# A fused attention and expert kernel whose first two tiles run interleaved, with a third start-up step of its own

## The reference, cut to what matters

```python
q, k, v = sigmoid(x @ Wq + bq), sigmoid(x @ Wk + bk), x @ Wv + bv       # by head
sink_in = normal / sum_d(q * cumsum(k)); src_out = normal / sum_d(k * cumsum(q))
cons_sink = sum_d(q * cumsum(k * src_out)) / normal
cons_src = clip(sum_d(k * cumsum(q * sink_in)) / normal, -1, 1)
vs = v * exp(cons_src) / cumsum(exp(cons_src)) * normal
kv = cumsum(outer(k, vs)); a = (q * sink_in / normal) . kv * sigmoid(cons_sink)
h = LN0(x + a @ Wo + bo); x1 = LN1(h + gelu(h @ W1 + b1) @ W2 + b2)
x2 = LN2(x + x1)
out = LN3(x2 + sum_e gate_e(x2) * (relu(x2 @ wi + bi + x2 @ A_e @ B_e) @ wo + bo))
```

## Time and profile before

| quantity | value |
|---|---|
| timed runs, median | 419.21 us (419.05 to 419.9) |
| the profiled execution, its own time | 418.39 us |
| its span in the trace | 416.6 us |
| PE (TensorE) busy | 374.6 us, 90% |
| DVE (VectorE) busy | 327.9 us, 79% |
| POOL (GpSimd) busy | 223.2 us, 54% |
| ACT (ScalarE) busy | 216.6 us, 52% |
| granted TensorE clock, mean | 0.99 |

### The profile page before, as it was taken

How to read it: one execution, slowest core, us unless ns; L and a number is a source line. 1 busy time by engine, 2 the same in 40 slices (tenths; PEclk the granted TensorE clock), 3 DMA queues, 4 the chain that set the end, 5 groups by cost and what they waited for, 6 DMA issues and landing times.

```text
span 416.6 us, 6454 instructions
## 1 busy us (share of the span) xinstructions
PE 374.6 (90%) x2082; PEld 261.3 (63%) x2082; DVE 327.9 (79%) x787; ACT 216.6 (52%) x399; POOL 223.2 (54%) x263
## 2 busy tenths in 40 slices
PE   8897789788998999989998999899989997799991
PEld 3555556465756875677657774778478765775551
DVE  3649966599589988999799979997899889832632
ACT  2240226327853586538852795278644874175541
POOL 2017234983279527963497348942795369735211
PEclk9999999899999999999999999999999999999997
DMA  8236006400180007300560028000810063000000
GB/s 257 115 71 158 1 2 152 125 3 0 37 217 2 0 2 183 97 0 2 116 162 2 0 56 223 3 0 16 204 36 0 2 160 68 0 1 27 12 14 25
DMA packets 19857, 26.58 MB, mean 64 GB/s; under 512 B 1648, under 2 KB 9968, under 8 KB 19824
## 3 DMA queue, kind: packets, MB, share of 16 engines
q1 hardware_dynamic: 19680, 25.96, 24.5%
q10 hardware_dynamic: 144, 0.21, 0.3%
HBM read 7.29 MB, written 2.10 MB: 23 GB/s over the span
## 4 chain that ended last, share of the span: by engine, by line
PE 31%; DVE 27%; POOL 19%; issue 14%; DMA 5%; ACT 2%; SPq 0%; POOLq 0%; DVEq 0%; ACTq 0%
POOL prod L848 12%; PE pB L354 5%; DMA vb<-vs 5%; DVE kv L1037 5%; PE pY L428 4%; PE pG L421 3%; DVE cum_kv L1043 3%; DVE cum_ks L937 2%; PE pG L497 2%; POOL rstd L838 2%; PE pG L490 2%; DVE cum_q L937 2%; PE pY L508 2%; DVE cum_qs L937 2%; DVE gel L1141 2%
## 5 line engine op out<-in xcount | busy, mean ns | idle before, releaser
L848 POOL TENSOR_TENSOR prod<-cum_kv,q_fac 128x512 f32<-128x512 f32 x64 | 94.5, 1483 | 33.9 <-DVE cum_kv L1043 25.7
L404 PEld LDWEIGHTS pO<-s_wor,prod 128*128 128x128 f32 x512 | 62.2, 191 | 33.5 <-POOL prod L848 21.4
L404 PE MATMUL pO<-s_wor,prod 128*128 128x128 f32 x512 | 69.5, 281 | 14.0 <-POOL prod L848 13.9
L1037 DVE TENSOR_TENSOR kv<-k,vb 128x512 f32<-128x512 f32 x64 | 52.8, 825 | 6.7 <-DMA vb<-vs 6.7
L835 POOL TENSOR_TENSOR var_eps<-mv,s_con 128x4 f32<-128x4 f32 x32 | 9.9, 310 | 71.1 <-DVE mv L1063 71.1
L1043 DVE TENSOR_TENSOR_SCAN cum_kv<-p_ones,cum_kv,kv 128x512 f32<-128x512 f32 x32 | 40.5, 1275 | 0.6
L1043 DVE TENSOR_TENSOR_SCAN cum_kv<-p_ones,kv 128x512 f32<-128x512 f32 x32 | 38.5, 1213 | 0.5
L657 ACT ACTIVATE v<-pA,s_att 128x512 f32<-128x512 f32 x7 | 4.8, 687 | 62.9 <-PE pA L340 62.9
L754 ACT ACTIVATE relu<-pG,s_att 128x512 f32<-128x512 f32 x28 | 19.2, 684 | 27.4 <-PE pG L490 27.4
L508 PEld LDWEIGHTS pY<-s_moe,gel 128*128 128x128 f32 x256 | 30.7, 192 | 3.7 <-issue 1.9
L508 PE MATMUL pY<-s_moe,gel 128*128 128x128 f32 x256 | 32.6, 276 | 0.0
(11 more groups left out here) (164 smaller groups left out, 772.7 us busy)
## 6 DMA issues: line engine op xcount, KB each, us to landing
vb<-vs SPq DMA_DIRECT2D x64, 256.0 KB, 4.7
xT<-x_t SPq DMA_DIRECT2D x8, 256.0 KB, 4.3
xt<-x SPq DMA_DIRECT2D x8, 256.0 KB, 5.3
out<-y SPq DMA_DIRECT2D x8, 256.0 KB, 2.3
s_moe<-moe_w SPq DMA_DIRECT2D x1, 836.0 KB, 10.4
s_wor<-wo_rep SPq DMA_DIRECT2D x1, 512.0 KB, 8.2
s_ffn<-ffn_w SPq DMA_DIRECT2D x1, 512.0 KB, 8.9
s_con<-consts SPq DMA_DIRECT2D x1, 502.0 KB, 4.4
```

Source lines behind the costliest of these rows:

```text
L404: mm = pe.matmul(pO3[:, s, :], prod[:, m % 4, s * P:(s + 1) * P], s_wor[:, m, :], start=False, stop=(m == DH - 1), skip_group_check=True)
L848: pool.tensor_tensor(prod[:, m % 4, :], cum_kv[t.par][:, m, :], q_fac[t.par][:, :], ALU.mult).then_inc(prod_ready, 1)
L1037: dve.tensor_tensor(kv[:, m % 3, :], k[t.par][:, :], vb[:, m, :], ALU.mult).then_inc(kv_ready, 1)
```

## The change

Tile 1's projections get banks of their own (pG[1] for q, pM for k and its first head sums), so its front need not wait for that of tile 0. The start now has three parts of its own. `opening` has tile 0's front and the beginning of tile 1's (up to its inverse denominators). `second_step` has the rest of tile 1's front beside tile 0's outer products, and no FFN. `third_step` has tile 2's front, tile 1's outer products, the FFN of tile 0 and that of tile 1, and tile 0's gate and first experts. It also takes over tile 2's outer products up to `outer_product(2, 5)` and `product(2, 2)`, which step 2 leaves out (`b.n > 2`). The common `step` begins at s=2. Tile 2's input is loaded at the end of the list of first transfers rather than later. Ten waits are added so that tiles interleaved in shared buffers don't overwrite each other. The fillers become 27 where there were 30.

```diff
+        def q_bank(t):
+            return pG[1] if t.n == 1 else pA
+        def k_bank(t):
+            return pM if t.n == 1 else pB
...
                 sp.wait_ge(vs_ready, t.n + 1)
+                wait(sp, kv_ready, DH * (t.n - 1) + m + 1)
...
+            load_xT(Tile(2))
...
             def project_q(t):
-                wait(pe, qfac_ready, t.n)
+                if t.n > 1:
+                    pe.wait_ge(qfac_ready, t.n)
...
             def project_v(t):
-                if t.n > 0:
+                if t.n == 1:
+                    pe.wait_ge(qfac_ready, t.n)
+                elif t.n > 1:
                     pe.wait_ge(q_ready, t.n + 1)
...
             def second_step(b):

                 a = b.plus(1)
+                keep_busy(1)
+                reduce_out(b, 1); reduce_out(b, 2)
+                keep_busy(1)
+                head_sums(a, 1, True)
+                reduce_out(b, 3)
+                keep_busy(1)
+                head_sums(a, 1, False)
...
+            def third_step(c):
+
+                b, a = c.plus(1), c.plus(2)
+                project_q(a); project_k(a)
...
+            def third_step(c):
+
+                b, a = c.plus(1), c.plus(2)
+                q_out(a); k_out(a)
+                normalise(c, 0); v_out(a); seed_x(b); h_out(c)
+                gelu(c, 0); gelu(c, 1)
+                seed_h(c)
+                gelu(c, 2); gelu(c, 3)
...
+                if B and b.n > 2: product(b, 1); product(b, 2)
...
-            step(Tile(-1))
+            opening(Tile(0))
             second_step(Tile(0))
-            run_steps(step, first=1, end=TILES)
+            third_step(Tile(0))
+            run_steps(step, first=2, end=TILES)
```

More of the change, by code:

```diff
@@ L312, in step @@
                 if B: spread_vs(b, 4); spread_vs(b, 5); spread_vs(b, 6)
-                if A and a.n == 2: load_xT(a)
                 if A and a.n >= 1: load_xt(a)
@@ L351, in head_sums @@
                 src, at = (kq, HW) if of_q else (qk, 0)
+                dst = k_bank(t) if pair == 0 else pB
                 for s in reversed(range(SUB)):
                     end = base + at + (s + 1) * HEADS
[L354 removed]
+                    mm = pe.matmul(dst[:, end - P:end], src[:, s * P:(s + 1) * P], wide_sum, start=True, stop=True)
                 mm.then_inc((den_ready, consp_ready)[pair], 1)
@@ L552, in second_step @@
                 a = b.plus(1)
+                keep_busy(1)
[3 more added lines that the diff above has]
+                reduce_out(b, 3)
+                keep_busy(1)
+                head_sums(a, 1, False)
+                reduce_out(b, 4)
                 keep_busy(2)
-                for m in range(1, 5):
-                    reduce_out(b, m)
-                head_sums(a, 0, True); head_sums(a, 0, False); project_v(a)
@@ L928, in _ @@
             second_step(Tile(0))
-            run_steps(step, first=1)
+            third_step(Tile(0))
+            run_steps(step, first=2)
         @block.vector
@@ L1174, in closing, with opening @@
                 expert_residual(c); moments(c, 3)
+            def opening(a):
+                b = a.plus(1)
+                cumulate_q(a); cumulate_k(a); k_times_cum_q(a, 0); q_times_cum_k(a, 0)
+                inverse_denominators(a); normal_denominators(a)
+                cumulate_q(b)
+                sink(a); cumulate_sink(a); source(a); k_times_cum_q(a, 1); cumulate_source(a); q_times_cum_k(a, 1)
+                cumulate_k(b)
+                k_times_cum_q(b, 0)
+                conserved(a); clip_source(a)
+                q_times_cum_k(b, 0)
+                prefix_e(a)
+                inverse_cum_e(a); source_factor(a); sink_factor(a)
+                values(a); query_factor(a)
+                inverse_denominators(b); normal_denominators(b)
+                outer_product(a, 0); cumulate_kv(a, 0); outer_product(a, 1)
             def second_step(b):
                 a = b.plus(1)
+                outer_product(b, 2); cumulate_kv(b, 1)
+                sink(a); cumulate_sink(a)
+                cumulate_kv(b, 2)
+                source(a); k_times_cum_q(a, 1); cumulate_source(a)
+                outer_product(b, 3); cumulate_kv(b, 3); outer_product(b, 4)
+                q_times_cum_k(a, 1)
+                cumulate_kv(b, 4); outer_product(b, 5)
+                conserved(a); clip_source(a)
+                cumulate_kv(b, 5); outer_product(b, 6)
+                prefix_e(a)
+                cumulate_kv(b, 6); outer_product(b, 7)
+                inverse_cum_e(a); source_factor(a); sink_factor(a)
+                cumulate_kv(b, 7)
+                values(a); query_factor(a)
                 dve.wait_ge(gb_loaded, 16)
@@ L1194, in second_step @@
                 values(a); query_factor(a)
-                outer_product(a, 0); cumulate_kv(a, 0); outer_product(a, 1); cumulate_kv(a, 1); outer_product(a, 2)
+                for i in range(6):
+                    gate(c, i)
+                sum_exp(c)
+                gate(c, 6); gate(c, 7); gate(c, 8); inverse_sum_exp(c); gate_total(c)
+                for i in range(9, GATE_STEPS):
+                    gate(c, i)
+                outer_product(a, 0); cumulate_kv(a, 0)
+                masked_lora(c, True); masked_lora(c, False)
+                outer_product(a, 1); cumulate_kv(a, 1); outer_product(a, 2); outer_product(a, 3); cumulate_kv(a, 2)
                 moments(b, 1)
-                outer_product(a, 3); cumulate_kv(a, 2)
+                second_relu(c, 0); second_relu(c, 1)
+                outer_product(a, 4); cumulate_kv(a, 3); cumulate_kv(a, 4); outer_product(a, 5)
                 moments(b, 2)
```

168 lines of the change are left out of this document (115 added, 53 removed).

## The result

The changed kernel takes **421.47 us** in the median (421.33 to 421.69), beside 419.14 us for the kernel before: a ratio of 1.0056, 95% interval 1.0039 to 1.0073. It is slower by 2.3 us. The forecast was 413.3 us, and the range ended at 418.5. The profiled execution took 421.33 us with a span of 419.5.

The account below looks back on a forecast made before the run. VectorE's order was taken to set the pace, its idle time being the start's loss. A tail ending 4.4 us earlier plus 1.5 regained in step 2 made 5.9 us less: 413.3 us, range 405.5 to 418.5.

Parts of the forecast that it names:

- 4.3 and 5.2 in the sum: VectorE's forecast waits in us: 4.3 in the second stage (to values(1)), 5.2 in the third (to tile 0's masked_lora).
- The opening: Start up to tile 1's denominators: forecast 0.9 us longer, with query_factor(0) ending at 27.7 instead of 26.8.
- I take 1.5: Step 2: TensorE's 1.5 us of idling for ScalarE and GpSimd is made up; bounds 0 and 1.5.
- the signs that were to show the prediction wrong: Stage to values(1) not shorter, granted clock under 0.9 over a whole stage, or full steps changed.
- I take 1.0, about half, since part of tile 1's kv already ran beside products.: Third stage: 1.0 us added because GpSimd and VectorE get in each other's way.
- The upper bound, 1.9 us: Third stage, GpSimd's hindrance of VectorE: at most 14 kv at the mean's excess of 0.14 us.
- The row of 1.76 us: A kv on VectorE beside a row of GpSimd products takes 1.76 us, against 0.69 alone.
- The other sum that the prediction named, 7.6 us more: Third stage at worst: each of tile 1's 8 kv pays 1.07 us, making the sum 7.6 higher.
- Sum 12.6, end at 115.1: Tail on TensorE, masks to end of reduce_out(2, 0): 12.6 us, ending at 115.1 instead of 119.5.
- rival C: Slower: TensorE's clock falls to 1.2 GHz; with the whole tail at it, 12.6 us more, 425.9; chance 0.10.
- there the half FFN of tile 1 stands behind `u_T(0)`: Tail on TensorE: two hidden (1.8 us) and four ffn_out (3.6) come after u_T(0), which follows masks forecast at 102.5.
- Rival B: Hand-over: tile 0's gate comes 3 us later, so the tail does too, 416.3 us; chance 0.13 (416 to 418.4).

Follow-up runs that it names:

- e11: Kernel before, plus three two-input GpSimd additions (128x512, into scratch nobody reads) where GpSimd was idle in its first step: ratio 1.0027 to the kernel before.
- e12: Kernel before, plus three GpSimd scalings (one input tile and a constant, 128x512) where GpSimd was idle: ratio 1.0007 to the kernel before.
- e4: Changed kernel with five matmul fillers in TensorE's idle 5.6 us ahead of u_T(0): ratio 1.0025 to the kernel before.
- e9: Changed kernel with u_T(0) behind tile 1's FFN, two GpSimd operations earlier, outer products directly behind scans, tile 2's head sums earlier: ratio 0.9886 to the kernel before.
- e3: Changed kernel with both u_T(0) moved behind tile 1's whole hidden and ffn_out on TensorE, ScalarE to match: ratio 0.9957 to the kernel before.

## Why the prediction was wrong

**What held.** The waits fell as reckoned. In the second and third stage VectorE waited 3.1 and 4.0 us for others in the waits that the view names, beside 4.3 and 5.2 in the sum (1.10 ahead of `conserved(1)`, where 1.6 was forecast; 1.28 for `values(2)`, where it was 1.1; none for `outer_residual(0)`). The opening was 0.7 us shorter than forecast, and the last row of step 1 to the denominators of tile 3 gave back 2.3 us, where "I take 1.5". Full steps kept their length (44.8 us from tile 3's denominators to tile 4's, 44.7 before). Of the signs that were to show the prediction wrong one came true: the granted clock was 0.89 over the second stage.

**What failed, first: "I take 1.0, about half, since part of tile 1's kv already ran beside products."** Measured: 7.0 us more than in the rows that the work was taken from in the third stage, and 2.7 in the second, which had no such term. They are most of what VectorE's busy time lies above the work reckoned (7.9 and 2.9 us), and so of the 6.7 and 2.2 us by which the stages are longer than forecast. In the second stage the clock decided a part: seven other executions with the same lists passed it in 1.1 to 1.3 us less. The upper bound, 1.9 us, came from a mean over 64 kv, many of which are issued right behind a scan, ahead of GpSimd's product. It isn't a bound for kv in a new order, and it left out everything that isn't kv: qk, kq, `clipped`, `e_pref` and the gate's small operations, 0.19 us each in step 1 of the kernel before because GpSimd was idle or at operations of 128x4 beside them (e11 makes one of them 1.25 by filling such a place). The row of 1.76 us was the right price, and the question was how often it would be paid. The other sum that the prediction named, 7.6 us more, for each of 8 kv, was nearer to the truth, by other instructions in part. The Trainium skill (SBUF — State Buffer, Who interferes with whom) says of VectorE's modes with two ports that whoever issues first gets the pair of ports shared with GpSimd for the whole instruction, and that the other blocks fully. The rows here, most of them of instructions with two inputs, agree beside GpSimd's additions and products, since an instruction of 0.19 us is held up for 1.0 as one of 0.69 us is; beside e12's scalings they do not (0.42 us at most). By that rule the term is a count of instructions behind a running one, and not a slowdown of a mean.

**Second: the tail, "Sum 12.6, end at 115.1".** Its terms had full speed. It took 14.1 us, and e4 puts 1.3 us of the time on the clock. The low clock was rival C's mechanism, at the tail as it said, but for part of it: it cost a tenth of rival C's price. What the step had right and the forecast didn't use was "there the half FFN of tile 1 stands behind `u_T(0)`". With masks at 102.5 us it would have left no idle time, since TensorE had other work until 105.2. With masks at 110.7 it puts 5.6 us of idle time into TensorE, while 5.4 us of matmuls that could have filled it (two `hidden` and four `ffn_out`) stay in the tail. Rival B (3 us from a late gate) priced that in series and stopped at 3 us; the gate was 8 us late.

**The arithmetic.** The next row after `reduce_out(2, 0)` starts at 124.7 instead of 115.1: 0.7 us less in the opening, 2.2 and 6.7 more in the two stages, 1.5 in the tail, together 9.7 (9.6 by the rows). Step 2 gave back 0.8 us more than forecast. That leaves 8.8 us, the distance from a gain of 5.9 to a loss of 2.9 in the profiled executions. Lists of the same work with both faults mostly mended (e9) give 414.4 us on the scale of the kernel before (0.9886 of 419.14), 1.1 above the forecast. That nearness is partly luck: e3's order takes those 5.4 us out of the tail, and the forecast's sum had them in it. It shows that a gain of the forecast's size was there to be had, not that the other terms were right.

**Open** is how much the second stage's collisions cost by themselves, and what the low clock costs in the executions that pass it in 29.4 us; no run took either away.
